# One graph layer on one core: transposed sums over windows that begin at a superblock's lowest destination, five slots with one-hots of their own, adds three pairs behind

## The reference

```
h = max(layernorm(x), 0)
msgs = sum_i where(type == i, h[src] @ W[i] + b[i], 0)
out = x + segment_sum(msgs, dst, 12500)
```

## Time and profile before

| | before |
|---|---|
| median of 3 runs | 2571.7 us (2563.07 to 2586.41) |
| profiled execution | 2568.76 us, span 2566.9 us |
| granted TensorE clock, mean of the span | 0.678 |
| POOL busy | 1477.0 us (58%) |
| PE busy, weight loads | 1202.5 us (47%), 981.1 us (38%) |
| DVE busy | 718.3 us (28%) |
| ACT busy | 134.8 us (5%) |
| DMA | mean 56 GB/s over the span |

### The profile page before, as it was taken

How to read it: one execution, slowest core, us unless ns; L and a number is a source line. 1 busy time by engine, 2 the same in 40 slices (tenths; PEclk the granted TensorE clock), 3 DMA queues, 4 the chain that set the end, 5 groups by cost and what they waited for, 6 DMA issues and landing times.

```text
span 2566.9 us, 23392 instructions
## 1 busy us (share of the span) xinstructions
PE 1202.5 (47%) x5394; PEld 981.1 (38%) x5395; DVE 718.3 (28%) x1591; ACT 134.8 (5%) x384; POOL 1477.0 (58%) x1575
## 2 busy tenths in 40 slices
PE   3249134434344454545445445445554344545455
PEld 1014133333332443344344334344444344444445
DVE  2038212222222222223323323233222222222223
ACT  1026000000000000000000000000000000000000
POOL 7730665565655556465565565655656666666663
PEclk7569566666676665656767766766677677667677
DMA  6337211111111111111111111111121111111211
GB/s 171 95 114 266 66 48 37 39 41 37 44 35 40 38 37 44 30 44 40 39 47 40 40 47 36 43 41 38 43 80 46 56 46 45 55 50 46 58 46 43
DMA packets 94971, 144.19 MB, mean 56 GB/s; under 512 B 27065, under 2 KB 57267, under 8 KB 94947
## 3 DMA queue, kind: packets, MB, share of 16 engines
q0 software_dynamic: 50016, 102.53, 14.0%
q1 hardware_dynamic: 40537, 39.02, 4.6%
q10 hardware_dynamic: 4394, 2.40, 0.3%
HBM read 111.76 MB, written 32.09 MB: 56 GB/s over the span
## 4 chain that ended last, share of the span: by engine, by line
another core or an unknown queue 41%; PE 24%; issue 18%; DVE 8%; DVEq 8%; ACT 0%; DMA 0%; ACTq 0%; SPq 0%; PEld 0%; PEldq 0%
PE ps_sum L693 15%; PE ps_y L720 4%; DVE onehot L576 3%; PE ps_y L648 3%; DVEq L229 2%; DVE acc L568 2%; DVEq L568 2%; PE ps_y L711 1%; DVEq L576 1%; DVE y L586 1%; PE ps_sum L729 1%; DVEq L572 1%; DVEq L594 1%; DVE y L504 0%
## 5 line engine op out<-in xcount | busy, mean ns | idle before, releaser
L341 POOL DMA_INDIRECT messages<-message_table,table_row x1443 | 1361.5, 944 | 1024.2 <-PEq L698 508.8
L693 PE MATMUL ps_sum<-messages,onehot 128*128 128x128 f32 x4438 | 872.8, 377 | 1075.6 <-DVE acc L568 452.6
L693 PEld LDWEIGHTS ps_sum<-messages,onehot 128*128 128x128 f32 x4438 | 812.1, 283 | 1135.4 <-issue 1072.8
L576 DVE SCALAR_TENSOR_TENSOR onehot<-ps_node,tile_base,dst_col 128x512 f32<-128x512 f32 x586 | 434.8, 749 | 1562.3 <-remote 880.4
L648 PE MATMUL ps_y<-w_sb,h_t 128*128 128x512 f32 x196 | 123.6, 727 | 97.7 <-issue 92.4
L720 PE MATMUL ps_y<-y 128*128 128x512 f32 x240 | 124.2, 670 | 56.0 <-DVE y L586 56.0
L329 POOL DMA_INDIRECT early_x<-in_x,src_col x120 | 113.4, 945 | 40.9 <-issue 39.3
L504 DVE TENSOR_TENSOR y<-ps_y,bias 128x512 f32<-128x512 f32 x98 | 67.3, 687 | 144.3 <-remote 112.4
L586 DVE SCALAR_TENSOR_TENSOR y<-ps_i,tile_base,key_col 128x1024 f32<-128x1024 f32 x60 | 75.1, 1279 | 114.9 <-remote 74.5
L720 PEld LDWEIGHTS ps_y<-y 128*128 128x128 f32 x240 | 49.5, 222 | 120.1 <-DVE y L586 69.4
L711 PE MATMUL ps_y<-onehot,type_mask 128*128 128x128 f32 x240 | 52.3, 406 | 83.0 <-DVE onehot L576 72.7
(11 more groups left out here) (64 smaller groups left out, 140.7 us busy)
## 6 DMA issues: line engine op xcount, KB each, us to landing
message_table<-y SPq DMA_DIRECT2D x98, 256.0 KB
messages<-message_table,table_row POOLq DMA_INDIRECT x1443
out<-acc SPq DMA_DIRECT2D x6, 896.0 KB
acc<-in_x SPq DMA_DIRECT2D x4, 896.0 KB
early_x<-in_x,src_col POOLq DMA_INDIRECT x120
acc<-in_x ACTq DMA_DIRECT2D x2, 896.0 KB, 5.5
acc<-in_x SPq DMA_DIRECT2D x1, 832.0 KB
src_rows<-in_src SPq DMA_DIRECT2D x1, 640.0 KB
```

Source lines behind the costliest of these rows:

```text
L341: pool.indirect_dma_start(messages[:, k, t, :], None, table_rows, bass.IndirectOffsetOnAxis(ap=flat_rows[:, at + t:at + t + 1], axis=0)).t ...
L576: nc.vector.scalar_tensor_tensor(out=onehot[:, a:z, :], in0=ps_node[:, :].unsqueeze(1).broadcast_to([P, z - a, P]), scalar=tile_base[:, ba ...
L693: ins = nc.tensor.matmul(ps_sum[:, bass.ds(q % 2, 1), 0:d], onehot[:, t, :], messages[:, k, t, :], start=(t == 0), stop=(t == tiles - 1))
```

## The change

The second stage is rebuilt; the first keeps its work.

- **Windows.** For superblocks 0 to 184 a pair no longer is an aligned node tile but a window of 128 destinations that begins at the superblock's lowest destination. A window can begin anywhere, so sums are made transposed: PE's stationary operand is the message tile and the moving one is the one-hot, and `acc` holds features by destinations, begins as zeros, and is added to at any column. The base of a window is worked out by a small DVE instruction and waited for.
- **Turn.** After superblock 184, DVE adds what is outstanding, clears the banks, PE transposes the 98 tiles back, and DVE adds `x` (loaded again into SBUF by SP after the last early superblock), four tiles at a time. The last 10 superblocks and the 3-tile one work as before, on aligned tiles.
- **Slots.** Five slots instead of four, each with one-hots of its own; early superblocks have theirs too. Early superblocks come after every 10 table superblocks.
- **Adds** run three pairs behind, over four PSUM banks. DVE makes the halves of the first window of a superblock without waiting for PE's signals.
- **Release.** PE frees a slot at the end of the next superblock, when all pairs before that one have signalled.
- **Ranges** also hold the lowest destination and the number of windows; a copy goes through HBM to all partitions.

The core of the diff:

```diff
-SLOTS = 4
+SLOTS = 5
+BANKS = 4
+LAG = 3
+OWN_ROUNDS = 2
+TURN = 4
+    window_rounds = rounds - OWN_ROUNDS
+    own_sbs = OWN_ROUNDS * SLOTS + 1
@@ sync
+            sp.dma_start(ranges_row..., ranges_by_chunk[:, :, :]...).then_inc(ranges_written, 16)
+            sp.wait_ge(ranges_written, 16)
+            sp.dma_start(all_ranges, ranges_row.broadcast_to([P, sbs * 4])).then_inc(ranges_everywhere, 16)
+            sp.wait_ge(e_used, EARLY_SBS + 1)
+            for at in range(0, node_tiles, GROUP):
+                sp.dma_start(x_rows[:, at:at + tiles, :], x[...]...).then_inc(x_reloaded, 16)
...
-            sp.wait_ge(sbs_passed, full_sbs + 2)
+            sp.wait_ge(sbs_passed, own_sbs + 1 + LAG)
@@ gpsimd
+            pool.wait_ge(lohi_ready, 2 * groups)
@@ vector
+            dve.wait_ge(h_ready, node_tiles)
+            nc.vector.memset(acc[:, :, :], 0.0).then_inc(acc_cleared, 1)
             dve.wait_ge(lohi_transposed, 2)
...
+            dve.wait_ge(ranges_everywhere, 16)
+            nc.vector.tensor_copy(window_lo, all_ranges...[:, :, 2]).then_inc(windows_ready, 1)
...
+            def make_onehot(s, home, tiles, base, needed):
+                for half, (a, z) in enumerate(halves(tiles)):
+                    dve.wait_ge(pair_done if half else first_half_done, needed)
+                    nc.vector.scalar_tensor_tensor(out=home[:, a:z, :], ..., scalar=base, ...
+                        op0=ALU.add, op1=ALU.is_equal).then_inc(onehot_ready[half], 1)
+            def next_pair(q):
+                add_sums(q, column_regs[LAG - 1]).then_inc(pair_added, 1)
+            def superblock(s, home, base_at, tiles, early=False):
+                first, windows, regs = load_windows(dve, s)
+                dve.reg_mov(column_reg, first)
+                dve.reg_mov(needed_reg, 1)
+                with dve.Fori(0, windows) as j:
+                    base = window_base[:, base_at:base_at + 1]
+                    nc.vector.tensor_tensor(base, window_lo[:, bass.ds(s, 1)], tile_base[:, bass.ds(j, 1)], ALU.add).then_inc(base_made, 1)
+                    dve.wait_ge(base_made, q)
+                    make_onehot(s, home, tiles, base, needed)
...
+                    next_pair(q)
+            def finish_windows():
+                for n in range(LAG):
+                    dve.wait_ge(pair_done, last + n)
+                    nc.vector.tensor_tensor(at, at, ps_sum[...], ALU.add).then_inc(last_window_added, 1)
+                nc.vector.memset(ps_sum[:, :, 0:d], 0.0).then_inc(windows_summed, 1)
+                dve.wait_ge(x_reloaded, (groups + 1) * 16)
+                for c, at in enumerate(range(0, node_tiles, TURN)):
+                    dve.wait_ge(tiles_turned, end)
+                    nc.vector.tensor_tensor(acc[:, at:end, :], x_rows[:, at:end, :], ps_y[:, c % 2, ...], ALU.add).then_inc(tiles_made, 1)
@@ tensor
+            def pairs_done_since(signal):
+                pe.wait_ge(pair_done, pe.snap(first_reg, ...) + (LAG - 1))
+                pe.sem_inc(signal, 1)
...
+                with pe.Fori(lo, hi):
+                    pe.wait_ge(gathered[k], needed)
+                    pe.wait_ge(pair_added, q)
+                    for half, (a, z) in enumerate(halves(tiles)):
+                        pe.wait_ge(onehot_ready[half], q)
+                        for t in range(a, z):
+                            still, moves = messages[k][:, t, :], onehots[k][:, t, :]
+                            if own:
+                                still, moves = moves, still
+                            ins = nc.tensor.matmul(ps_sum[:, bass.ds(q % BANKS, 1), 0:d], still, moves, ...)
+                        ins.then_inc(pair_done if half else first_half_done, 1)
+                if frees is not None:
+                    pairs_done_since(slot_free[frees])
-                pe.wait_ge(half_free, count() * 2 + 2)
-                pe.sem_inc(slot_free[k], 1)
...
+            def turn_tiles():
+                pe.wait_ge(windows_summed, 1)
+                for n in range(node_tiles):
+                    wait(pe, tiles_made, n // TURN - 1)
+                    nc.tensor.transpose(ps_y[...], acc[:, n, :], ident[:, :]).then_inc(tiles_turned, 1)
```

More of the change, by code:

```diff
@@ L75, in sem @@
         return nc.alloc_semaphore(name)
-    acc = sb("acc", [P, node_tiles, d])
+    assert EARLY_SBS * EARLY_ROUNDS < window_rounds and node_tiles <= early_tiles and d == P
+    acc = sb("acc", [P, node_tiles + 1, d])
     table_row = sb("table_row", [P, chunks, P], I32)
@@ L196, in gnn_program @@
     key_onehot_free = sem("key_onehot_free")
-    h_sums_done = sem("h_sums_done")
     h_sums_ready = sem("h_sums_ready")
-    onehot_ready = sem("onehot_ready")
-    half_free = sem("half_free")
+    onehot_ready = [sem(f"onehot_ready{half}") for half in range(2)]
+    first_half_done = sem("first_half_done")
+    pair_done = sem("pair_done")
     pair_added = sem("pair_added")
@@ L563, in add_sums @@
[L563 to L581 removed]
+            needed_reg = dve.alloc_register("dve_pairs_needed")
@@ new lines, in _, with add_sums @@
+            column_reg, _ = counter(dve, "column")
+            column_regs = [counter(dve, f"column_{n}_before")[0] for n in range(1, LAG + 1)]
+            def add_sums(q, before, ahead=0):
+                column = dve.snap(before, min_val=0, max_val=node_tiles * P - 1)
+                dve.wait_ge(pair_added, q + ahead)
+                dve.wait_ge(pair_done, q + ahead)
+                at = flat_acc[:, bass.ds(column, P)]
+                return nc.vector.tensor_tensor(at, at, ps_sum[:, bass.ds((q + (1 + ahead)) % BANKS, 1), 0:d], ALU.add)
@@ L615, in _, with early_norm @@
                     nc.vector.bn_aggr(e_mean_var[:, t, :], e_stats[:, t, :]).then_inc(e_mean_var_ready, 1)
[L616 removed]
+            def early_norm(i):
                 dve.wait_ge(e_std_ready, i + 1)
@@ L686, in superblock @@
+            def superblock(s, k, tiles, needed, frees, own):
+                if own:
+                    lo, hi, regs = load_range(pe, s)
+                else:
+                    first, hi, regs = load_windows(pe, s)
+                    lo = 0
+                pe.reg_mov(first_reg, pair_reg)
                 with pe.Fori(lo, hi):
-                    q = count()
+                    q = pair()
                     pe.wait_ge(gathered[k], needed)
-                    pe.wait_ge(pair_added, q + 1)
+                    pe.wait_ge(pair_added, q)
@@ L690, in superblock @@
                     for half, (a, z) in enumerate(halves(tiles)):
-                        pe.wait_ge(onehot_ready, q * 2 + (half + 1))
+                        pe.wait_ge(onehot_ready[half], q)
                         for t in range(a, z):
-                            ins = nc.tensor.matmul(ps_sum[:, bass.ds(q % 2, 1), 0:d], onehot[:, t, :],
-                                                   messages[:, k, t, :], start=(t == 0), stop=(t == tiles - 1))
-                        ins.then_inc(half_free, 1)
@@ L696, in superblock @@
-                    pe.reg_add(q_reg, q_reg, 1)
-                pe.wait_ge(half_free, count() * 2 + 2)
-                pe.sem_inc(slot_free[k], 1)
+                            still, moves = messages[k][:, t, :], onehots[k][:, t, :]
+                            if own:
+                                still, moves = moves, still
+                            ins = nc.tensor.matmul(ps_sum[:, bass.ds(q % BANKS, 1), 0:d], still, moves,
+                                                   start=(t == 0), stop=(t == tiles - 1))
```

274 lines of the change are left out of this document (174 added, 100 removed).

## The result

The changed kernel takes 2452.7 us in the median of five runs (2435.2 to 2456.4), the kernel before 2568.8 in five beside them; the ratio of the two is 0.952 (95%: 0.949 to 0.955). That is 4.8% less, where 2.2% was forecast. The profiled execution took 2435.2 us. The first two lines are from its page.

What follows compares the result with a forecast made beforehand. PE's signals, held back while gathers stream and let through by POOL's pauses, were taken to set the cadence. 276.9 + 174 x 11.15 + 150 + 5 + 33 + 8.6 + 74 + 24 + 1.9 = 2513 us; range 2350 to 2630.

Steps and rivals of the forecast that it cites:

- A delay of POOL by DVE instructions with two SBUF inputs: Second stage, 185 window-base instructions: by the skill's rule up to 31 us added; forecast as nothing.
- The cadence: POOL's gathers in the second stage: bursts of four superblocks, pause 4.9, 11.15 us per superblock instead of 11.6, gaining 78 us.
- the first rival: Second-stage depth doesn't help: cadence stays 11.6, early superblocks 12.2, start and turn paid on top, 2625 us; chance 0.2.
- the early superblocks: Early superblocks among the table superblocks: 10 us each instead of 12.2, 15 x 10 = 150 us, gaining 33 us.
- the third rival: Second-stage depth hides everything, POOL doesn't pause, 10.0 us per superblock: 2238 us, anything up to 2450 included; chance 0.18.
- The turn: After superblock 184: 5 us pause, 33 us of adds, memset and transposes, then 8.6 us until a slot is free.
- first gather: Start of the second stage: clearing acc adds 11.8 us, so the first gather comes at 276.9 us.
- gathers behind the turn: Last superblocks after the turn: 51 gathers at 1.45 us, 74 us.
- the end: From the last gather to the kernel's end: 24 us, like now.
- POOL's wait for PE: POOL waiting for PE to free slots: down from 508.8 to about 400 us.
- bursts of 32: Second-stage gathers in the trace after: come in bursts of 32, with pauses of 4 to 5 us.
- the hole of 45 us: At the turn: a gap of about 45 us in the gathers near 2370.

Runs made afterwards that it cites:

- 240 columns: 128x240 memset on POOL behind every gather: changed kernel, accumulators cleared after the ranges, 2252.8 us (1.143); kernel before 2252.9 us (1.143); both on a free chip.
- the kernel with matmuls only: Changed kernel's second stage cut to gathers plus eight PE matmuls per slot, the last one's signal freeing it, aggregation left out: 2350.7 us (0.901).

## Why the prediction was half right

**Direction and diagnosis held.** PE's signals are held while gathers stream, POOL's pause lets them through, and DVE's waits moved to the adds. The larger number of pairs before, the windows' base (185 x 0.160 us) and the reload of x show no cost where POOL's issue is the bound: with gathers every 1.43 us on a free chip the two kernels take the same time. On a held chip they were not undone one by one. A delay of POOL by DVE instructions with two SBUF inputs would have shown as gathers further apart than 1.25 us. In the kernel with adds one pair behind, on the free chip, there are 185 such instructions, and the longest of the 1442 intervals between gathers is 1.27 us. The prediction cited the Trainium skill for this rival (SBUF — State Buffer, Who interferes with whom); the same section also says that `tensor_tensor` was seen not to stall DMAs, and this trace agrees.

**The cadence failed.** "A pause of 4.9 between the rows of three and five" took the pause as levelling off. It grows by 1.2 us per superblock. The row that misled, 5.20 us behind five, is from the first burst of the stage; even a bare stream of gathers runs unhindered only for its first 190. In steady state a cycle of four costs 45.5 us and the floor of any n is 11.2. The bursts were shorter than forecast as well: of 78, five were of four superblocks, 29 of three, 24 of two and 19 of one. Measured 11.48 for 11.15: 174 x 0.33 = 57 us more than forecast. By its cadence the result is all but the first rival, which was to decide from 11.5 up; only the early superblocks set it apart. The end of 10.0 us for the third rival could not be reached on such a chip; a free one reaches it (1.248 us a gather).

**The early superblocks failed the other way, and this is the error that made the gain twice the forecast.** "10 us each" was the stretch from the held signals to the superblock's end (502.2 to 512.2), with POOL taken to stand still for all of it. That gave the depth to the cadence alone. But the depth can't go below the floor; what it hides is a superblock that keeps PE longer. Measured 2.2: 15 x 7.8 = 117 us less than forecast. The undone parts show that without the slot, the distance of the adds or the late release it is 8.8 to 10.4, and the kernel before with a fifth slot shows 12.3.

**The turn was too dear.** It was put at 5 + 33 + 8.6 = 46.6 us; the hole in the gathers is 20.3. The turn itself took 20.4 us (2305.99 to 2326.4), not 31: 25 chunks at 0.82, as the adds (687 ns) overlap the transposes. The next gather is 7.9 us behind it, as forecast (8.6). And eight gathers ran from 2304.4 to 2314.1, most of them beside it.

**The rest** was near: first gather 278.5 for 276.9, gathers behind the turn 78.5 for 74, the end 20.5 for 24. Together 2513 + 57 - 117 - 26 + 1.6 + 4.5 - 3.5 = 2430, against 2435. Errors of opposite sign hid part of each other. The direction was right, but not for the reason given first: of the gain, the forecast gave 78 us to the cadence and 33 to the early superblocks, and the two traces show about 42 (174 x 0.24) and 143 (15 x 9.5). Of the signs named, the first gather (278.5) and the move of DVE's waits came, POOL's wait for PE fell to 347 us for about 400, and bursts of 32 and the hole of 45 us did not come.

## What to carry to other kernels

When a producer pauses for longer after longer bursts, plot cycle against burst length before trusting any single pause: a straight line through nearly zero points to a rate limit, and deeper buffers won't beat it. They hide the uneven work instead, so cost them there, and look at slots, distance of the consumers and point of release together: here each was worth little without the others. Where issuing too fast holds somebody else's signals, try to slow the issuer to just above the interval that is taken; but measure on more than one chip, as the same kernel ran 24% faster on a chip without the effect, and there a milder spacing (240 columns) costs 14%.

## What was not expected of the hardware

- Held and free chips: the kernel before took 2569 to 2610 us in four sets of runs and 1971 in two; beside the same early gathers the first stage passes 16 or 97 tiles in 130 us.
- On held chips an indirect gather of 128 rows of 512 B is taken every 1.40 us in steady state; issued faster for over some 190 gathers, most of POOL's instructions grow from 0.94 to 1.09 us. The data still lands promptly: the last packet ends 2.1 to 2.3 us after the issue, as on free chips.
- On held chips, with gathers issued faster than that, signals of PE's matmuls are late (9.3 us in the median, 20 and more at worst), and in the kernel with matmuls only the matmuls themselves start 2.80 us apart. Kernels in which DVE or plain semaphore increments of PE free the slots show no such pauses. At 1.494 us between gathers the median signal is 0.01 us late.
